# Scatters of edge records straight from the record buffer, GpSimd's program written out

## The reference

```python
scores = jnp.sum(q[src] * k[dest], axis=-1) / jnp.sqrt(D) + attention_mask   # edge_attr_8
ex = jnp.exp(scores - segment_max(scores, src)[src])
weights = ex / segment_sum(ex, src)[src]
out = segment_sum(v[src] * weights[:, :, None], dest) @ Wo.T + bo
x = layernorm(x + out)
h = silu(concat([x[row], x[col], edge_attr_2]) @ eW1 + eb1)
agg = segment_sum(silu(h @ eW2 + eb2), row)
x = layernorm(x + silu(concat([x, agg]) @ nW1 + nb1) @ nW2 + nb2)
```

## Time and profile before

| | us |
|---|---|
| median of three runs | 5489.91 |
| lowest and highest | 5485.45, 5490.59 |
| span of the profiled execution | 5485.4 |
| first scatter starts | 160.33 |
| last scatter ends | 1328.12 |
| first load of the next stage | 1338.98 |
| GpSimd busy in scatters of the stage (784) | 779.2 |
| GpSimd busy in copies of the stage (784) | 182.6 |

### The profile page before, as it was taken

The page is one execution under the profiler, slowest core; times in us unless marked ns, Lnnn a source line. Parts: engine busy times, 40 slices in busy tenths (PEclk is TensorE's granted clock), DMA queues, the critical chain, the costliest instruction groups (busy, mean ns, idle before and its releaser), DMA issues. The chain is left out here.

```text
span 5485.4 us, 85482 instructions
## 1 busy us (share of the span) xinstructions
PE 2866.4 (52%) x21791; PEld 2562.0 (47%) x21792; DVE 2423.9 (44%) x6521; ACT 779.2 (14%) x1649; POOL 4120.0 (75%) x5002
## 2 busy tenths in 40 slices
PE   6444444442333333331565666666653577778776
PEld 5333333331333333331455555555553466677765
DVE  7655555552333333336533333333333644444445
ACT  0111111110000000000111111111111322222222
POOL 1688888886888888883588888888886377777773
PEclk9666666665555555555787778787786799999999
DMA  2300000001222222220243444444445433333333
GB/s 85 110 11 11 10 11 11 11 10 68 72 72 71 69 72 70 70 71 21 24 35 35 35 35 35 35 35 35 35 35 94 120 78 77 77 78 76 78 76 82
DMA packets 301449, 293.46 MB, mean 53 GB/s; under 512 B 62976, under 2 KB 240570, under 8 KB 300377
## 3 DMA queue, kind: packets, MB, share of 16 engines
q0 software_dynamic: 201376, 176.66, 20.7%
q1 hardware_dynamic: 100024, 116.22, 7.2%
HBM read 198.74 MB, written 93.92 MB: 53 GB/s over the span
## 5 line engine op out<-in xcount | busy, mean ns | idle before, releaser
L1106 POOL DMA_INDIRECT sums_dram<-we_merged_rows,we_idx x832 | 1289.7, 1550 | 385.3 <-issue 204.6
L1685 POOL DMA_INDIRECT ed_bg<-b_rows_dram,ed_idx x832 | 808.7, 972 | 262.5 <-issue 240.7
L800 POOL DMA_INDIRECT sc_k<-k_rows_dram,sc_idx x832 | 827.1, 994 | 145.3 <-POOL sc_idx L789 130.4
L640 POOL DMA_INDIRECT records_dram<-rec_out,row_idx x784 | 779.2, 994 | 207.9 <-POOL rec_out L627 164.4
L900 PE MATMUL ps_q<-tab,sc_oht 128*128 x1664 | 386.5, 426 | 740.8 <-DVE sc_oht L813 740.8
L900 PEld LDWEIGHTS ps_q<-tab,sc_oht 128*128 128x128 f32 x1664 | 358.8, 327 | 772.3 <-issue 772.3
L1257 PE MATMUL ps_merged<-we_rows,we_same_dst 128*128 128x129 f32 x1664 | 337.7, 366 | 585.2 <-issue 428.9
L1257 PEld LDWEIGHTS ps_merged<-we_rows,we_same_dst 128*128 128x128 f32 x1664 | 288.9, 261 | 620.9 <-issue 611.4
L1159 DVE SCALAR_TENSOR_TENSOR we_firsts<-we_merged_rows,lane_unmark,two_marks 128x4 f32<-128x4 f32 x208 | 46.3, 222 | 1012.6 <-ACT we_merged_rows L1202 1012.6
L828 DVE TENSOR_TENSOR sc_prods<-ps_q,sc_k 128x1024 f32<-128x1024 f32 x104 | 127.3, 1224 | 745.3 <-DMA sc_k<-k_rows_dram,sc_idx 745.3
L1719 DVE TENSOR_TENSOR vals<-vals,ps_ed_s 128x128 f32 x832 | 238.9, 287 | 391.8 <-PE ps_ed_s L1816 296.7
(11 more groups left out here) (307 smaller groups left out, 6534.6 us busy)
## 6 DMA issues: line engine op xcount, KB each, us to landing
sc_lane_rows<-lanes_dram SPq DMA_DIRECT2D x104, 256.0 KB, 3.4
ed_lane_rows<-lanes_dram SPq DMA_DIRECT2D x104, 256.0 KB
sc_k<-k_rows_dram,sc_idx POOLq DMA_INDIRECT x832, 2.5
sums_dram<-we_merged_rows,we_idx POOLq DMA_INDIRECT x832, 3.3
ed_bg<-b_rows_dram,ed_idx POOLq DMA_INDIRECT x832
sums_dram<-zero_rows SPq DMA_DIRECT2D x20, 640.0 KB, 8.7
records_dram<-rec_out,row_idx POOLq DMA_INDIRECT x784
mi_rows<-sums_dram SPq DMA_DIRECT2D x48, 256.0 KB, 4.5
```

The costliest lines, as they stand in the source:

```text
L640: pool.indirect_dma_start(c.rec_rows, bass.IndirectOffsetOnAxis(ap=idx[:, b, j:j + 1], axis=0), out[:, b, j, :], None, bounds_check=SLOTS ...
L800: pool.indirect_dma_start(kg[:, r, k * F:(k + 1) * F], None, c.k_dram[:, :], bass.IndirectOffsetOnAxis(ap=idx[:, r, k, C_DST:C_DST + 1], a ...
L1106: pool.indirect_dma_start(c.acc_dram[k][:, :], bass.IndirectOffsetOnAxis(ap=idx[:, r, k:k + 1], axis=0), rows[:, r, k, 0:F], None, compute ...
L1685: pool.indirect_dma_start(bg[:, r, k * F:(k + 1) * F], None, c.b_dram[:, :], bass.IndirectOffsetOnAxis(ap=idx[:, r, k:k + 1], axis=0)).the ...
```

## The change

GpSimd's program for the stage is written out as a plain sequence over all 98 batches: 98 waits for the index of a batch, and 784 scatters. A scatter reads its records in place, from `e.rec`, at a fixed address. The ring `out`, its copies, their semaphore and the `scatter_turn` count go away. `idx` has room for all 98 batches, so that neither VectorE nor GpSimd waits any more for scatters that have been sent; only at the end of the stage does GpSimd wait for all of them. VectorE's, TensorE's, ScalarE's and SyncE's programs stay loops.

```diff
--- before.py
+++ after.py
@@ -366,11 +366,10 @@
 
     nc = c.nc
     names = ("place_onehot_n place_onehot_w place_turned place_onehot_t place_gram place_earlier place_table_kept "
-             "place_counted place_slots masked slot slot_int slot_tile slot_scaled slot_lane slot_chunk slot_line row_index rec_slot")
+             "place_counted place_slots masked slot slot_int slot_tile slot_scaled slot_lane slot_chunk slot_line row_index")
     (s_ohl, s_ohw, s_tr, s_lt, s_gram, s_gm, s_tab, s_hist, s_slots, s_msk, s_red, s_int, s_tile, s_mul, s_lane, s_chunk,
-     s_line, s_idx, s_rec) = semaphores(nc, c.sems, names)
+     s_line, s_idx) = semaphores(nc, c.sems, names)
     s_sent = semaphores(nc, c.stack, "records_sent0 records_sent1")
-    (s_turn,) = semaphores(nc, c.sems, "scatter_turn")
     (s_x, s_kout, s_w, s_bias, s_parts, s_mm, s_qv, s_k) = semaphores(
         nc, c.sems, "x_in k_out w_in qkv_bias place_parts qkv_ready qv_read k_read")
     with ExitStack() as t:
@@ -389,8 +388,7 @@
         chunk = sb("slot_chunk_i", [P, PG], I32)
         lane = sb("slot_lane_f", [P, PG], F32)
         line = sb("slot_line_f", [P, PG], F32)
-        idx = sb("row_idx", [P, 2, PG], I32)
-        out = sb("rec_out", [P, 2, PG, R], F32)
+        idx = sb("row_idx", [P, IT, PG], I32)
         w = sb("w_qkv", [P, 3 * F], F32)
         bias = sb("b_qkv", [P, 3 * F], F32)
         bp = sb("b_qkv_parts", [P, 3, 3 * F], BF16)
@@ -495,8 +493,7 @@
                                              op0=ALU.mult, op1=ALU.add).then_inc(s_line, 1)
                     dve.wait_ge(s_chunk, g + 1)
                     dve.wait_ge(s_line, g + 1)
-                    wait_count(dve, s_sent[b], 16 * PG * i)
-                    dve.scalar_tensor_tensor(out=idx[:, b, :], in0=chunk[:, :], scalar=-float(NT - 1), in1=line[:, :],
+                    dve.scalar_tensor_tensor(out=idx[:, bass.ds(g, 1), :].rearrange("p g k -> p (g k)"), in0=chunk[:, :], scalar=-float(NT - 1), in1=line[:, :],
                                              op0=ALU.mult, op1=ALU.add).then_inc(s_idx, 1)
 
                 def step(i, b):
@@ -623,24 +620,13 @@
             def _(pool):
                 pool.wait_ge(c.s_rfill, 16 * (NT // RF))
 
-                def record(g, b, j):
-                    pool.tensor_copy(out[:, b, j, :], e.rec[:, bass.ds(g * PG + j, 1), :].rearrange("p t r -> p (t r)")
-                                     ).then_inc(s_rec, 1)
-
-                def send(i, b):
-                    g = 2 * i + b
-                    wait_count(pool, s_sent[b], 16 * PG * i)
-                    record(g, b, 0)
+                for g in range(IT):
                     pool.wait_ge(s_idx, g + 1)
                     for j in range(PG):
-                        if j + 1 < PG:
-                            record(g, b, j + 1)
-                        pool.wait_ge(s_rec, PG * g + j + 1)
-                        pool.sem_inc(s_turn, 1)
                         pool.indirect_dma_start(
-                            c.rec_rows, bass.IndirectOffsetOnAxis(ap=idx[:, b, j:j + 1], axis=0),
-                            out[:, b, j, :], None, bounds_check=SLOTS - 1, oob_is_err=False).then_inc(s_sent[b], 16)
-                each_pair(pool, send)
+                            c.rec_rows, bass.IndirectOffsetOnAxis(ap=idx[:, g, j:j + 1], axis=0),
+                            e.rec[:, g * PG + j, :], None, bounds_check=SLOTS - 1, oob_is_err=False
+                        ).then_inc(s_sent[g % 2], 16)
                 for b in range(2):
                     pool.wait_ge(s_sent[b], 16 * PG * (IT // 2))
```

## The result

The changed kernel took 5408.78 us (median of four, 5405.07 to 5410.07) beside 5487.68 for the kernel before: ratio 0.9853, interval [0.9839, 0.9867], 79 us less. Forecast were 5343 and at most 5376. The direction was right, the size a little over half of what was said.

What follows compares the result with a forecast made beforehand. GpSimd was taken to bound the placing stage; 98 batches at 10.39 us would end it at 1181.5 instead of 1328.12, 146.6 us sooner, so 5489.91 becomes 5343 us. Range 5308 to 5376.

Steps and rivals of the forecast that it cites:

- The bound: Placing stage: GpSimd sets the pace and stays last; VectorE, running free, is done near 830 us.
- B: GpSimd's written-out program: fetching its instructions adds stalls; a dozen would be 28 us, giving 5371; 7%.
- C: Gap between scatters shrinks, a scatter costs 0.98 us, total falls to about 5095; 3%.
- D: Chain of VectorE, TensorE and ScalarE needs over 11.9 us a batch, so time stays at 5490; 2%.
- odd gaps: Six gaps of about 2.3 us in GpSimd's placing stage before the change, 0.12 us a batch.
- The pattern: GpSimd's placing stage: scatter after scatter, 0.994 us plus a 0.305 gap, 1.299 each, 10.39 a batch.
- the sum: End of the placing stage: 174.0 + 97 x 10.39 - 0.3 = 1181.5 us, against 1328.12 before.
- For the instruction itself I keep its own mean here, 0.994 us: Scatter's duration in the placing stage, taken unchanged from the mean before the change.
- Rival A: VectorE's SBUF instructions L222, L453, L457, L459 block scatters for their full length, 1.84 us a batch: 5510, slower; 4%.
- each of 98 batches loses 0.35 us: Worse bound: loss to VectorE instead of 0.14 us (20 us), 14 us of gaps stay: 5378.
- its sign, a mean over 1.1 us: Scatter L640's mean rising over 1.1 us would show that blocking by VectorE has a part.

Runs made afterwards that it cites:

- psum_iota_act: Changed kernel with one-hot builders reading node numbers from PSUM, and ScalarE doing the row copy L451 and cast L455: 5348.89 us, ratio 0.9751.
- psum_iota_b: Changed kernel with the one-hot builders L222 and L216 reading the row of node numbers from PSUM: 5350.76 us, ratio 0.9752.
- act_keeps_b: Changed kernel with row copy L451 and cast L455 done by ScalarE, and subtraction L457 moved behind L466: 5355.15 us, ratio 0.9760.
- copies_written: Kernel before with only GpSimd's program written out; copies, ring, two index halves and VectorE's wait kept: 5488.61 us, ratio 1.0005.
- two_onehots_b: Changed kernel with the one-hot L222 made twice per batch: 5366.11 us, ratio 0.9779.

## Why the prediction was wrong

**The bound: right.** GpSimd last, VectorE early (861.9 us, forecast 800 to 850), no DMA wait at L496, 10.8 us to the next stage. Rivals B, C and D didn't come about: instruction fetches rose from 27 to 36 on one queue and stayed at 22 on the other; there are six odd gaps of 1.3 to 1.7 us, about as many as before; the usual gap between scatters is 0.305.

**The pattern: right.** A scatter alone is 0.972 and the next comes 1.277 us after it. Were that all, the stage would end at 174.62 + 776 x 1.277 - 0.3 = 1165. The forecast's 1181.5 has 17 us of disturbance in it (784 x 0.022). psum_iota_act, with 10 us of stretch and the odd gaps, ends at 1182.5 and takes 5349 where 5343 was forecast: that kernel, not the changed one, is what the sum describes.

**The failing step: "For the instruction itself I keep its own mean here, 0.994 us, which has the disturbances by VectorE in it."** Measured 1.059: 0.065 x 784 = 51 of the 60 us missing in the stage. The other nine: 0.6 at the start, 0.315 in place of 0.305 for the gaps (8). The mean of before was taken under a VectorE that a landing released in every batch: L222 then starts in the turn of the same scatter of the batch in 90 of 95 batches, and over the stage only 23 scatters meet L222, 22 meet L459 (L457 of the changed kernel) and none L216. In the changed kernel these are 45, 88 and 87. Part of the disturbance of before was also in the copies (243 ns to 214), which I counted as gained. Free, VectorE and GpSimd fall into step.

**Rival A: right in kind, wrong in size.** Blocking costs 0.69 us a batch, under the 1.5 from which it would have decided. It was given 4% and a full-length price, and nothing between 0.35 and 1.84 us a batch was considered: "each of 98 batches loses 0.35 us" was the worst that I allowed. Nothing in the rows of before excluded more, since its collisions were those of another order of work. Its list of instructions was wrong too: L216 (0.855 us, two inputs in SBUF) was left out and made 11 of the 68 us, while L453 and L457 of before (L451 and L455 here) made next to none. And its sign, a mean over 1.1 us, stood too high: the mean was 1.059 with rival A at work.

**After the stage.** Of 86.6 us, 82.1 arrived in the span. In the scoring stage the 832 gathers of L786 have a mean of 1002 ns in place of 994, 7 us; psum_iota_b has 1003, act_keeps_b 1002, and copies_written 996. Why is open. The medians differ by 79.

## What to carry to other kernels

A scatter of GpSimd waited for the end of a VectorE instruction with two inputs in SBUF that had begun before it. So VectorE is not off the path while GpSimd bounds the stage, however early it is done. One input in PSUM took the block away, even where the instruction got longer by it (5407 to 5351 us). A shorter batch of VectorE, with part of its work on ScalarE, gained nearly as much (5355).

The loss isn't chance. Two engines that meet in a repeating pattern can fall into step, and then the slower pattern sets the pace of both. Count the one's instructions in the other's period, and price a collision by a trace with the same order of work. When a wait goes that kept two engines in phase, the mean durations measured under it don't hold any more.

## What the runs showed of the hardware that I had not expected

- A held scatter is longer by what is left of VectorE's instruction 0.13 us after the scatter's start: stretch 0.369 us by a mean rest of 0.366 of L457, over 88 scatters. L216 lets go a little before its end (0.127 us by 0.177). Which of the two began first decides: the cast L458 of two_onehots_b, begun just after the scatter's start, cost 77 scatters 0.002 us each.
- L216 in bf16 (0.855 us) blocks as L222 does, and with a float32 input from PSUM it takes 0.575 us and doesn't. A reduction from SBUF (one input, 0.56 us) doesn't block: 90 scatters in act_keeps_b. The table's cast (L455) blocks when it began before the scatter, but the traces of this chip speed have only six such cases (mean 0.103 us by a rest of 0.103).
- The block goes both ways: beside scatters the cast L481 takes 0.280 us in place of 0.172, at most 0.464.
- The lock in step held with ten scatters at pairs of 13.08, 13.94, 14.34 and 15.30 us, and went over to twelve at 15.73, where the second L222 was added.
- On two chips of those that ran the kernels, the one before took 5820 and 5897 us in place of 5487, and five variants of the changed kernel that are 0.6 to 2.5% faster than the kernel before elsewhere were 1.6 to 2.8% slower there.
